# Attention scores of two heads at once, stacked at partitions 0 and 64, with a fourth bank for max scores

## The chip, the cores and the metric

The kernel runs on one core of one Trainium2 chip, in one launch. The metric is the device time in microseconds (us), taken as the median of several runs; lower is better.

## The reference

The input x is 8 batches of 512 tokens with 256 features. One transformer layer is computed in fp32: causal attention with 16 heads of size 16 beside a gated memory path, a layer norm, then a mixture of 8 experts (top 2 of 10, two of them null), and another layer norm. What the change touches is the attention alone:

```python
scores = jnp.einsum('bhtd,bhsd->bhts', q, k) * scale      # 8 batches, 16 heads, 512 x 512
scores = jnp.where(causal, -jnp.inf, scores)
attn = jax.nn.softmax(scores, axis=-1)
seq_out = jnp.einsum('bhts,bhsd->bhtd', attn, v)
```

## The kernel before

Three stages follow each other: an opening (weights, the first batch's projections, memory lines of all batches), eight attention batches, and a last stage with the experts.

**Stacks.** TensorE multiplies in a rounded type (fp32r). For fp32 accuracy each q and k is split in a high and a low part, and q·k is hi·hi + hi·lo + lo·hi. The parts are stacked along partitions: tile `Q` holds (hi, hi, lo) and tile `K` holds (hi, lo, hi), 3 x 16 = 48 rows of a head, zeros up to row 95 (`STACK = 96`), and in rows 96 and 97 `Q` has the row maxima (high and low part) and `K` has -1. One head is one matmul, with 96 rows (max scores) or 98 rows (exp scores, which subtract the maximum).

**Groups and units.** A batch is 4 groups of 4 heads; a group is 12 units (`unit_parts`, L285). Units 0 to 3 are one head with 512 key columns each, 4 to 7 one head with 384, 8 and 9 two heads with 256, 10 and 11 two heads with 128 (done as 256). Each unit is computed twice:

- `pe_max_scores` (L305) computes q·k with queries on partitions into one of three PSUM banks (`S_ps`, `u % 3`), and `dve_max` (L459) adds the mask and takes the row maximum. It may start unit u when unit u-3 has been read (`s_max`, L311). It runs 8 units (`LEAD`) plus one group ahead of the exp scores.
- The 16 columns of maxima of a group are turned by `pe_turn_max` (L354), split into high and low part by `dve_turned_max` (L483, tile `MT`), and written into rows 96 and 97 of `Q` by two DMAs (`sp_max_rows`, L640). The first exp unit of the group waits for them (`s_mrow`, L322).
- `pe_exp_scores` (L318) computes k·q into one of two banks (`ST_ps`, `u % 2`), and `act_exp` (L403) takes the exponential into `Pr`. It may start unit u when the exp of unit u-2 is done (L323). GpSimd masks the diagonal (`pool_mask`, L608), and `pe_values` (L331) multiplies with V for the group before, at units 0, 2, 4, 6. Its four heads go to four 32-column strips of the output and its operands are plain fp32.

**Beside it.** Each group carries two of the next batch's eight projection steps (`pe_project`, L360): six matmuls into bank `J_ps`, at units 4 and 10; `act_project` (L413) and `dve_project` (L473, at units 5 and 11) evacuate it. Steps 0 to 3 give q and k parts in the single tile `HL`, stored to DRAM (`sp_projected`, L620) and loaded back as stacks with six DMAs a group (`sp_stack`, L628); `act_project` writes `HL` only after the step before has been stored. Steps 4 to 7 give v and the memory value (`Vn`, `MV`). `act_out` (L424, unit 7), `pe_turn_out` (L343) and `dve_normalise` (L495), both at unit 10, finish the outputs of the group before. `act_split_x` and `dve_split_x` (L435, L508) split the next batch's x at unit 0 of group 0. From batch 2 to batch 6 VectorE also runs 36 scans of the memory path (`dve_scan`, L512), three in two groups of three (`SCAN_AT`, L548), at units 6, 8, 10 and then 0, 2, 4.

Every engine runs a list of its own in program order; they meet at semaphores alone. TensorE's order is `pe_batch` (L381): for each unit exp scores, max scores, values, project, turn max, turn out.

## Time and profile before

| | before |
|---|---|
| median of 3 runs | 833.69 us (831.81 to 835.61) |
| the profiled execution, device time | 833.96 us |
| its span, first to last instruction | 832.2 us |
| TensorE busy (modelled) | 745.5 us, 90% |
| VectorE busy | 592.8 us, 71% |
| ScalarE busy | 354.1 us, 43% |
| GpSimd busy | 443.3 us, 53% |
| mean granted TensorE clock | 0.936 of 2.4 GHz |
| opening / attention / last stage | 0 to 77.9 / 77.9 to 544.6 / 544.6 to 832.2 us |

The attention stage is counted from the first exponential of batch 0 to the end of the last exponential of batch 7. "Busy" of TensorE counts a matmul from its start to its modelled end; overlapping matmuls make it say little on pace, which is read from the distance between starts. PEld rows are weight loads. A row of the order of time gives start and length in us, then engine, line, operation, tiles, shape, and how many like instructions were merged (x2); in square brackets stands the engine's idle time before it and what ended that.

### The profile page before, as it was taken

Reading aid. Unit: us, or ns where it says so; the run is one execution under the profiler, and the core shown is the slowest. Engines: PE = TensorE matmul, PEld = TensorE weight load, DVE = VectorE, ACT = ScalarE, POOL = GpSimd, SP = SyncE. Lnnn points to the kernel's source line nnn. Section 1 sums busy time; section 2 is a strip of 40 time slices with the busy share of each in tenths; the row PEclk is TensorE's granted clock in tenths of the full one; section 3 lists DMA queues with packets and bytes.
Section 4 is the critical chain, followed back from the end, with each engine's and each line's share of the span. In section 5 each row is a group of like instructions: output and inputs, shape, how many; then the busy total and the mean of one; then the engine's idle time right before and its main releaser. Section 6 shows DMA issues by size and latency. Waiting matters only on the chain.

```text
span 832.2 us, 12627 instructions
## 1 busy us (share of the span) xinstructions
PE 745.5 (90%) x4116; PEld 519.1 (62%) x4116; DVE 592.8 (71%) x2089; ACT 354.1 (43%) x709; POOL 443.3 (53%) x350
## 2 busy tenths in 40 slices
PE   6994998998898999999889998878999999999995
PEld 3552665566465565565555664557788787887884
DVE  2344776778887888888788776635767777677685
ACT  2211555555454455555455465732242342332410
POOL 9200994995676666667475891524254153341510
PEclk9995999999998999999999996979999999999998
DMA  7899599574654655756564556030220302303000
GB/s 272 263 235 175 125 138 144 154 122 97 156 82 96 154 84 112 159 90 146 110 96 112 121 88 214 8 102 0 77 86 18 102 11 91 102 2 102 26 26 26
DMA packets 60421, 89.89 MB, mean 108 GB/s; under 512 B 8234, under 2 KB 37316, under 8 KB 60356
## 3 DMA queue, kind: packets, MB, share of 16 engines
q1 hardware_dynamic: 60356, 89.09, 47.5%
q8 instruction: 33, 0.54, 0.3%
q14 instruction: 32, 0.26, 0.1%
HBM read 54.72 MB, written 33.82 MB: 106 GB/s over the span
## 4 chain that ended last, share of the span: by engine, by line
PE 58%; DVE 18%; DMA 7%; POOL 6%; ACT 5%; issue 4%; SPq 2%; ACTq 0%; POOLq 0%; DVEq 0%
PE ps L1246 21%; PE ps L374 10%; PE ps L338 7%; PE ps L327 7%; PE ps L315 6%; DMA Q<-MT 5%; DVE ps L468 5%; DVE Ob L516 3%; PE ps L232 2%; PE ps L1212 2%; ACT X L1232 1%; DVE Z L1266 1%; ACT Pr L411 1%; PE ps L351 1%; DVE HL L477 1%
## 5 line engine op out<-in xcount | busy, mean ns | idle before, releaser
L468 DVE CUSTOM_DVE_ANT_0 ps<-ps,mask 128x256 f32<-128x256 f32 (+3 forms) x512 | 236.6, 509 | 29.4 <-PE ps L315 28.8
L411 ACT ACTIVATE Pr<-ps 128x512 f32<-128x512 f32 (+2 forms) x384 | 190.1, 527 | 112.3 <-PE ps L327 108.2
L327 PE MATMUL ps<-Q,K 98*128 98x256 f32 (+2 forms) x512 | 172.3, 379 | 27.2 <-DMA Q<-MT 20.0
L1246 PE MATMUL ps<-ew_hi,XT 128*128 128x512 f32 x512 | 181.4, 416 | 0.0
L315 PE MATMUL ps<-K,Q 96*128 96x256 f32 (+2 forms) x512 | 156.9, 352 | 23.2 <-DVE nmax L468 22.8
L1372 DVE SCALAR_TENSOR_TENSOR A<-ps,cw,A 128x256 f32<-128x256 f32 x256 | 123.6, 483 | 54.1 <-PE ps L1246 42.7
L327 PEld LDWEIGHTS ps<-Q,K 98*128 98x128 f32 x512 | 93.7, 196 | 102.0 <-ACT Pr L411 60.4
L612 POOL TENSOR_SCALAR_AFFINE_SELECT Pr<-Pr 128x512 f32<-128x512 f32 x128 | 88.6, 706 | 100.8 <-ACT Pr L411 98.4
L315 PEld LDWEIGHTS ps<-K,Q 96*128 96x128 f32 x512 | 101.6, 201 | 45.0 <-DVE nmax L468 28.6
L1246 PEld LDWEIGHTS ps<-ew_hi,XT 128*128 128x128 f32 x512 | 101.3, 198 | 21.8
L1246 PE MATMUL ps<-ew_rest,XT 128*128 128x512 f32 x256 | 104.8, 409 | 0.0
L338 PE MATMUL ps<-Pr,V 128*17 128x512 f32 (+3 forms) x1024 | 98.0, 458 | 1.7 <-POOL Pr L612 1.7
L1186 POOL TENSOR_TENSOR A<-A,X 128x512 f32<-128x512 f32 x16 | 20.6, 1287 | 94.8 <-ACT A L1238 94.8
L468 DVE DVE_READ_ACCUMULATOR2_ANT nmax<- 128x1 f32 x512 | 69.5, 136 | 0.0
L1246 PEld LDWEIGHTS ps<-ew_rest,XT 128*128 128x128 f32 x256 | 50.8, 198 | 9.4
L419 ACT ACTIVATE HL<-ps,qkb 128x512 fp32r<-128x512 f32 x32 | 22.0, 687 | 80.5 <-PE ps L374 55.8
L801 POOL TENSOR_TENSOR Ob<-Wm 128x511 f32<-128x511 f32 (+1 forms) x12 | 14.2, 1187 | 66.2 <-DMA Wm<-mem_scratch 66.0
L852 POOL TENSOR_TENSOR Ob<-Ob,Rl 128x1533 f32<-128x1533 f32 x12 | 34.8, 2903 | 27.4 <-DVE Ob L516 27.4
L374 PE MATMUL ps<-xhi,wqk 128*128 128x512 f32 x128 | 47.3, 454 | 1.8 <-DVE HL L477 1.5
L516 DVE TENSOR_TENSOR_SCAN Ob<-sc,Ob 128x512 f32<-128x512 f32 x36 | 45.7, 1269 | 0.0
L854 POOL TENSOR_TENSOR Wm<-Wm,Ob 128x1533 f32<-128x1533 f32 x12 | 43.3, 3609 | 0.9
L374 PE MATMUL ps<-wvc,xhi 128*128 128x512 f32 x128 | 42.8, 415 | 0.4 <-DVE bc L945 0.4
(187 smaller groups left out, 1115.8 us busy)
## 6 DMA issues: line engine op xcount, KB each, us to landing
qk_scratch<-HL SPq DMA_DIRECT2D x32, 512.0 KB, 3.2
Q<-qk_scratch SPq DMA_DIRECT2D x96, 128.0 KB, 4.3
K<-qk_scratch SPq DMA_DIRECT2D x96, 128.0 KB, 5.6
Pr<-xT SPq DMA_DIRECT2D x8, 512.0 KB, 6.0
xraw<-xT SPq DMA_DIRECT2D x8, 512.0 KB, 6.4
mem_scratch<-Rl SPq DMA_DIRECT2D x16, 256.0 KB, 6.6
mv_scratch<-MV SPq DMA_DIRECT2D x32, 128.0 KB, 1.7
Wm<-mem_scratch SPq DMA_DIRECT2D x16, 256.0 KB, 9.3
```

What stands on the lines that cost most here:

```text
L315: last = nc.tensor.matmul(o, Q[0:STACK, hh, P * i:P * i + P], K[0:STACK, hh, 0:n], start=True, stop=True)
L327: last = nc.tensor.matmul(o, K[0:STACK + 2, hh, P * kt:P * kt + P], Q[0:STACK + 2, hh, T - n:T], start=True, stop=True)
L338: last = nc.tensor.matmul(O_ps[32 * h:32 * h + VW, P * kt:T], V[:, kt, GROUP * g + h, :], probs(g % 2, kt, h, 1)[:, 0, :], start=(kt == 0) ...
L374: last = nc.tensor.matmul(J_ps[:], lhs, rhs, start=first, stop=(j < 4 and k == KT - 1 and a == 1))
L411: nc.scalar.activation(probs(g % 2, kt, heads[0], len(heads)), src, ACT.Exp, scale=SCALE).then_inc(s_exp, 1)
L468: last = nc.vector.tensor_tensor_reduce(out=scores, in0=scores, in1=mask[:, T - w:T], scale=1.0, scalar=NEG, op0=ALU.add, op1=ALU.max, acc ...
L516: nc.vector.tensor_tensor_scan(Ob[:, j % 3, :], col(SC_D).to_broadcast([P, T]), Ob[:, j % 3, :], 0.0, ALU.mult, ALU.add).then_inc(s_scan, 1)
L612: nc.gpsimd.affine_select(out=diagonal, in_=diagonal, compare_op=ALU.is_ge, fill=0.0, base=0, pattern=[[0, GROUP], [1, P]], channel_multip ...
L852: step(nc.gpsimd.tensor_tensor(Ob[:, :, 0:T - 1], Ob[:, :, 0:T - 1], Rl[:, i:i + 1, 1:T].to_broadcast([P, 3, T - 1]), ALU.mult))
L854: step(nc.gpsimd.tensor_tensor(Wm[:, lo:lo + 3, 0:T - 1], Wm[:, lo:lo + 3, 0:T - 1], Ob[:, :, 0:T - 1], ALU.add))
L1246: last = nc.tensor.matmul(o, lhs(c, k), rhs(d, k), start=first, stop=(k == KT - 1 and c == 1))
L1372: ins = nc.vector.scalar_tensor_tensor(acc, F_ps[v % 4][:, D * c:D * c + D], cw[:, par, i, e:e + 1], acc, ALU.mult, ALU.add)
```

## The change

- `STACK` becomes 48 and the zero rows go. `Q` and `K` hold two heads on top of each other: even heads at partitions 0 to 49, odd heads at partitions 64 to 113 (`HALF = 64`), each with its two rows of maxima at 48 and 49 of its half. The tiles have half as many columns. A new tile `later` is allocated ahead of them and not used in this stage.
- `pe_max_scores` and `pe_exp_scores` are called every second unit and issue two units u and u+1, one matmul from each half in turn, so that two neighbouring matmuls use different halves of the rows and different banks. Units 8 to 11 pair heads 0 and 2, 1 and 3.
- Max scores have four banks (0, 1, 7, 5). The turned output goes to the bank of `O_ps` and the turned maxima to that of `J_ps`; the waits follow the new owners: a project step waits for the copy of the turned maxima, the turned maxima for the end of the last project step, and the values of a group for the normalised output of the last.
- The exp scores of a pair wait until the exponentials of both units before it are done (`s_exp` of `UNITS * g + u`, where it was `u - 1`).
- Project steps are at units 0 and 8 (they were at 4 and 10), evacuated by ScalarE after units 1 and 9 and by VectorE at units 3 and 11. The turned output is at unit 8, ahead of the project step, and `dve_normalise` at unit 9; `dve_turned_max` is at unit 5.
- The split of x for batch b+2 is at the end of batch b (that of batch 1 ahead of batch 0).
- The DRAM layout of q and k has the parts inside the head. A projected tile is stored with two DMAs, high and low part apart. A group's stacks are loaded with eight DMAs (they were six), with the same bytes; its maxima with four (they were two).
- GpSimd's opening memsets cover 64 rows of `K` in place of 96 rows of `Q` and `K`.

```diff
-STACK = 96
+STACK = 48
+HALF = 64
-        S_ps, ST_ps = ps[0:2] + ps[7:8], ps[2:4]
-        O_ps, OT_ps, J_ps = ps[4:7]
-        M_ps = OT_ps
+        S_ps, ST_ps = [ps[0], ps[1], ps[7], ps[5]], ps[2:4]
+        O_ps, J_ps = ps[4], ps[6]
+        OT_ps, M_ps = O_ps, J_ps
...
+        def stacked(t, hh, n):
+
+            return t[HALF * (hh % 2):HALF * (hh % 2) + n, hh // 2, :]
...
         def pe_max_scores(pe, b, g, u):
...
             need(pe, s_max, PU, b, UNITS * g + u - 2)
-            for c, h in enumerate(heads):
-                hh = GROUP * g + h
-                o = S_ps[u % 3][:, c * 256:c * 256 + n]
-                last = nc.tensor.matmul(o, Q[0:STACK, hh, P * i:P * i + P], K[0:STACK, hh, 0:n], start=True, stop=True)
-            last.then_inc(s_s, 1)
+            for c in range(len(unit_parts(u)[1])):
+                for v in (u, u + 1):
+                    rank, heads = unit_parts(v)
+                    i, hh = QT - 1 - rank, GROUP * g + heads[c]
+                    n = max(P * (i + 1), 2 * P)
+                    ins = nc.tensor.matmul(S_ps[v % 4][:, c * 256:c * 256 + n], stacked(Q, hh, STACK)[:, P * i:P * i + P],
+                                           stacked(K, hh, STACK)[:, 0:n], start=True, stop=True)
+                    if c == len(heads) - 1:
+                        ins.then_inc(s_s, 1)
...
-            need(pe, s_exp, PU, b, UNITS * g + u - 1)
+            need(pe, s_exp, PU, b, UNITS * g + u)
...
-                for u in range(UNITS):
+                for u in range(0, UNITS, 2):
                     pe_exp_scores(pe, b, g, u)
                     on, ng, nu = ahead(g, u)
                     if not (last and on):
                         pe_max_scores(pe, b + on, ng, nu)
-                    if u in (0, 2, 4, 6) and not (first and g == 0):
+                    if u < 8 and not (first and g == 0):
                         pe_values(pe, pb, pg, u // 2)
-                    if u in (4, 10) and not last:
-                        pe_project(pe, b + 1, 2 * g + u // 10)
+                    if u == 8 and not (first and g == 0):
+                        pe_turn_out(pe, pb, pg)
+                    if u in (0, 8) and not last:
+                        pe_project(pe, b + 1, 2 * g + u // 8, NG * b + g + 1 + u // 8)
...
-                    if g == 0 and u == 0 and not last:
-                        act_split_x(act, b + 1)
-                    if u in (4, 10) and not last:
-                        act_project(act, b + 1, 2 * g + u // 10)
+                    if u in (1, 9) and not last:
+                        act_project(act, b + 1, 2 * g + u // 9)
+                    if (g, u) == (NG - 1, 10) and b < NB - 2:
+                        act_split_x(act, b + 2)
...
             for r in range(2):
-                sp.dma_start(Q[STACK + r:STACK + r + 1, GROUP * g:GROUP * g + GROUP, :].rearrange(
-                    "o h (i t) -> o (h i) t", i=QT).bitcast(F32), MT[:, g % 2, r, :].bitcast(F32)).then_inc(s_mrow[g], 16)
+                for a in range(2):
+                    row = HALF * a + STACK + r
+                    sp.dma_start(Q[row:row + 1, 2 * g:2 * g + 2, :].rearrange("o c (i t) -> o (c i) t", i=QT).bitcast(F32),
+                                 MT[2 * QT * a:2 * QT * a + 2 * QT, g % 2, r, :].bitcast(F32)).then_inc(s_mrow[g], 16)
```

## Rows read from the trace of the kernel before

**Rows 1.** Stretches (us, busy us by engine, clock, DMA share): batches 0, 1, 2 to 6, 7
```profile
core 0: us, PE busy (x) PEld busy (x) DVE busy (x) ACT busy (x) POOL busy (x), PEclk, DMA share, GB/s
77.93:133.80 55.87, 51.89 (x294) 35.06 (x293) 39.75 (x160) 30.10 (x61) 43.62 (x39) 0.92 0.78 134
133.80:191.02 57.22, 53.00 (x330) 33.90 (x328) 42.46 (x166) 30.64 (x62) 48.66 (x41) 0.97 0.69 130
191.02:489.42 298.40, 271.93 (x1642) 174.45 (x1640) 245.57 (x867) 154.21 (x310) 201.36 (x125) 0.95 0.57 115
489.42:544.57 55.15, 47.89 (x302) 27.49 (x304) 39.43 (x142) 35.99 (x72) 25.07 (x25) 0.85 0.41 105
```
**Rows 2.** Stretches: groups 0 and 2 of batch 6
```profile
430.34:447.65 17.31, 14.48 (x83) 9.04 (x81) 13.73 (x45) 9.40 (x18) 12.66 (x7) 0.90 0.45 86
...
463.48:476.44 12.96, 12.66 (x85) 8.37 (x83) 9.70 (x43) 6.96 (x16) 9.84 (x8) 1.00 0.63 114
```
**Rows 3.** TensorE's longest wait, attention stage: total us, times, longest us
```profile
PE ps L315 <- DVE nmax L468: 20.8, 36, 2.3
```
**Rows 4.** Order of time, batch 6 group 2: TensorE and ScalarE
```profile
463.55 1.05 PE L338 MATMUL ps<-Pr,V 128*17 128x512 f32 x8
...
464.53 0.19 PEld L327 LDWEIGHTS ps<-Q,K 98*128 98x128 f32 x1 [0.85 <-ACT Pr L411]
...
464.87 0.41 PE L315 MATMUL ps<-K,Q 96*128 96x256 f32 x2
...
465.06 1.08 ACT L411 ACTIVATE Pr<-ps 128x512 f32<-128x512 f32 x2 [0.99 <-PE ps L327]
...
465.11 0.40 PE L327 MATMUL ps<-Q,K 98*128 98x512 f32 x1
...
465.34 0.40 PE L315 MATMUL ps<-K,Q 96*128 96x256 f32 x2
...
465.67 0.13 PEld L338 LDWEIGHTS ps<-Pr,V 128*17 128x17 f32 x8
...
470.18 0.90 ACT L411 ACTIVATE Pr<-ps 128x384 f32<-128x384 f32 x2
...
471.07 0.19 PEld L327 LDWEIGHTS ps<-Q,K 98*128 98x128 f32 x1 [0.21 <-issue]
...
471.55 0.49 ACT L411 ACTIVATE Pr<-ps 128x384 f32<-128x384 f32 x1 [0.46 <-PE ps L327]
...
472.09 0.30 PEld L327 LDWEIGHTS ps<-Q,K 98*128 98x128 f32 x2 [0.19 <-ACT Pr L411]
...
474.98 0.48 PEld L351 LDWEIGHTS ps<-ident,Osb 128*128 128x128 f32 x4
...
475.43 0.30 PEld L327 LDWEIGHTS ps<-Q,K 98*128 98x128 f32 x2
```
**Rows 5.** Groups of instructions (busy us, mean ns, idle before), attention stage, ScalarE
```profile
L419 ACT ACTIVATE HL<-ps,qkb 128x512 fp32r<-128x512 f32 x28 | 19.2, 687 | 69.5 <-PE ps L374 53.0 <-DMA qk_scratch<-HL 16.5
L427 ACT ACTIVATE Osb<-ps 128x512 f32<-128x512 f32 x31 | 18.4, 592 | 0.0
...
L438 ACT ACTIVATE xhi<-xraw 128x1024 fp32r<-128x1024 f32 x7 | 7.3, 1049 | 0.0
```
**Rows 6.** Order of time, batch 6 group 0: the split of x on VectorE
```profile
433.47 2.63 DVE L510 TENSOR_TENSOR xlo<-xraw,xhi 128x1024 fp32r<-128x1024 f32 x1
...
437.03 0.47 PE L315 MATMUL ps<-K,Q 96*128 96x512 f32 x1 [2.30 <-DVE nmax L468]
```
**Rows 7.** TensorE's longest wait at the opening's end, 60 to 80 us
```profile
PE ps L327 <- DMA Q<-MT: 9.5, 1, 9.5
```
**Rows 8.** Order of time, batch 6 group 2: SyncE issues the maxima's DMAs
```profile
470.69 1.14 SPq L643 DMA_DIRECT2D Q<-MT  x2
```
**Rows 9.** The same DMAs in the whole attention stage: issue to landing
```profile
DMA to landing us min/median/max: 1.8/2.8/7.8
```

More of the change, by code:

```diff
@@ L217, in opening @@
                 project(j)
[L218 removed]
+                scores(*((0, 4), (4, 6), (6, 10), (10, 12))[j - 4])
             memory(16)
@@ L318, in pe_exp_scores @@
         def pe_exp_scores(pe, b, g, u):
-            kt, heads = unit_parts(u)
-            n = max(T - P * kt, 2 * P)
             if u == 0:
-                need(pe, s_mrow[g], 32, b, 32)
-            need(pe, s_exp, PU, b, UNITS * g + u - 1)
-            for c, h in enumerate(heads):
-                hh = GROUP * g + h
-                o = ST_ps[u % 2][:, c * 256:c * 256 + n]
-                last = nc.tensor.matmul(o, K[0:STACK + 2, hh, P * kt:P * kt + P], Q[0:STACK + 2, hh, T - n:T],
-                                        start=True, stop=True)
@@ L329, in pe_exp_scores @@
-            last.then_inc(s_st, 1)
+                need(pe, s_mrow[g], 64, b, 64)
+            need(pe, s_exp, PU, b, UNITS * g + u)
+            for c in range(len(unit_parts(u)[1])):
+                for v in (u, u + 1):
+                    kt, heads = unit_parts(v)
+                    hh = GROUP * g + heads[c]
+                    n = max(T - P * kt, 2 * P)
+                    ins = nc.tensor.matmul(ST_ps[v % 2][:, c * 256:c * 256 + n],
+                                           stacked(K, hh, STACK + 2)[:, P * kt:P * kt + P],
+                                           stacked(Q, hh, STACK + 2)[:, T - n:T], start=True, stop=True)
+                    if c == len(heads) - 1:
+                        ins.then_inc(s_st, 1)
@@ L364, in pe_project @@
             need(pe, s_lo, 8, b, j)
+            need(pe, s_mt, 2, turned, 0)
             first = True
@@ L730, in mem_rows @@
                         "(w h) t -> h w t", h=H)).then_inc(s_mw[c], 16)
-            opening(project, lambda i: sp_memory(sp, i), lambda: None, lambda u: None)
+            opening(project, lambda i: sp_memory(sp, i), lambda: None, lambda u0, u1: None)
             for i in range(6):
@@ L951, in project, with scores @@
                 dve_project(dve, 0, j)
-            def scores(u0):
+            def scores(u0, u1):
                 if u0 == 0:
-                    dve.wait_ge(s_cst, 2)
-                for u in range(u0, u0 + 3):
+                    dve.wait_ge(s_cst, 1)
+                for u in range(u0, u1):
                     dve_max(dve, 0, 0, u)
@@ L995, in fold @@
                 for k in range(KT):
-                    last = nc.tensor.matmul(OT_ps[:, 0:D], mb_bc[:, k, :], wst_ow[:, k, :],
+                    last = nc.tensor.matmul(S_ps[3][:, 0:D], mb_bc[:, k, :], wst_ow[:, k, :],
                                             start=(k == 0), stop=(k == KT - 1))
@@ L1011, in scores @@
                     pe.wait_ge(s_wr, 4)
-                for u in range(u0, u0 + 3):
+                for u in range(u0, u1, 2):
                     pe_max_scores(pe, 0, 0, u)
@@ L1018, in _ @@
             pe.wait_ge(s_p1g, 2)
-            pe_turn_max(pe, 0, 0)
-            for u in range(LEAD):
+            pe_turn_max(pe, 0, 0, 8)
+            for u in range(0, LEAD, 2):
                 pe_max_scores(pe, 0, 1, u)
```

112 lines of the change are left out of this document (58 added, 54 removed).

## The prediction

> **What bounds the kernel now.** I read the stretches first. The attention stage is 466.6 of the 832.2 us of span, and the change reaches little else. Its five middle batches take 298.40 us, 59.7 each; batches 0, 1 and 7 take 55.87, 57.22 and 55.15 [rows 1]. In a group that nothing disturbs TensorE is busy for 12.66 of 12.96 us and VectorE for 9.70, ScalarE for 6.96 [rows 2]. So a clean group is bound by TensorE's issue, and four of them would be 51.8 us. What is above that is stalls: 7.9 us in a middle batch, 5.4 in batch 1, 4.0 in batch 0, 3.3 in batch 7. Group 0 of batch 6, with 17.31 us, shows the kind [rows 2]. TensorE's largest wait there and in the stage as a whole is for VectorE's maxima to free a bank, 20.8 us in 36 waits [rows 3]. VectorE is busy for 245.57 of the 298.40 us of the middle batches, 49.1 us a batch, since the scans fall there [rows 1]: it is the second bound, close behind.
>
> Then I read one clean group in order of time for the pace of TensorE [rows 4]. Starts after a matmul of 512 columns are 0.23 us apart (465.11 to 465.34), two of 256 columns take 0.24 (464.87 to 465.11), 0.12 each. Where the array is empty the weight load shows: from the load at 464.53 to the next matmul at 464.87 is 0.34, so 0.11 of load and 0.23 of stream. The eight value matmuls, four heads in four column strips with plain fp32 operands, take 0.98 (463.55 to 464.53) and are in flight together: this is concurrency in the array, but of columns, not of rows. From the last score matmul (started at 465.34 + 0.12, 0.11 of stream) to the load for the values at 465.67 is 0.10, which I take as the drain when the use of the array changes.
>
> **What the change removes.** A group has 16 exp and 16 max matmuls: 4 of 512 columns, 4 of 384, 8 of 256 each. By the paces above, with 0.17 for 384 as the mean of its neighbours, that is 2 x (0.92 + 0.68 + 0.96) = 5.1 us. If two halves run at once it is 2.6. The trace of before has no row of two row halves. The nearest, the values, speak for full overlap; the other end is none. I take full overlap, of the weight loads too, and keep the other end for the range. The Trainium skill (TensorEngine Tiling (Array Packing), Tiling Modes) says that tiles of 64 rows load and multiply in parallel; by it the sum is the one I take.
>
> **What it adds: a lockstep.** Before, the exp scores of unit u waited for the exp of u-2, so TensorE filled one bank while ScalarE read the other. Now a pair waits for both exps of the pair before. Behind that wait stand max scores, values and project steps. So a group is six rounds, and each is the longer of two chains.
>
> ScalarE's chain: from the load to the start of the exp 0.53 (464.53 to 465.06), two exps of 512 in 1.08, and from the exp's end (471.55 + 0.49) to the next load at 472.09 another 0.05: 1.66 us. With 384 columns: 0.48 (471.07 to 471.55) + 0.90 + 0.05 = 1.43. Two of 256: exps of 512 and 384 are 0.60 and 0.49, so 0.38 each and 0.67 a pair is my estimate, 1.25 in all [rows 4].
>
> TensorE's chain rules where there is a project step. Round 0: load 0.11, one exp step 0.23, two max steps 0.24, drain 0.10, values 0.98, project 0.11 + 6 x 0.23 = 1.49, drain 0.10: 3.25. Rounds 2, 4, 6 have values and max scores in the shadow of ScalarE's 1.66, 1.43, 1.43. Round 8: the copy of the output on ScalarE 0.59 [rows 5], the turned output 0.45 (474.98 to 475.43) [rows 4], project 1.49, drain 0.10: 2.63. Round 10: 1.25. ScalarE's evacuation of a q or k step, 0.69 [rows 5], comes ahead of the exps in rounds 2 and 10 and outlasts the 0.53 by 0.16; that of v and memory values is half as wide and hides, but such a step has one more matmul, 0.12. Groups 0 and 1: 3.25 + 1.82 + 1.43 + 1.43 + 2.63 + 1.41 = 11.97. Groups 2 and 3: 3.37 + 1.66 + 1.43 + 1.43 + 2.75 + 1.25 = 11.89. The split on ScalarE, 1.05 [rows 5], now stands in round 10 of group 3, uncovered. A batch: 2 x 11.97 + 2 x 11.89 + 1.05 = 48.8 us where it was 51.8. So of 2.5 us of matmul time a group only 0.8 to 1.1 comes back; the rest is idle time in the lockstep.
>
> **The stalls.** (a) The split of x on VectorE, 2.63 us long, held up max scores, and TensorE lost 2.30 [rows 6], with the granted clock at 0.90 in that group (full is 2.4 GHz, the mean has stretches at 1.2) against 1.00 [rows 2]. It now comes ahead of a round of 3.25 us with two max pairs in store. I take 3.0 us a batch away, 2.0 in batch 0, where it moves into the wait of 9.5 us for the first maxima [rows 7]. If that cover is gone, it costs them again. (b) New: VectorE evacuates the project step of round 8 at unit 11, and TensorE wants the bank 1.7 us into the next group; `HL` must be stored before ScalarE writes it at unit 1, where it had until unit 4. Both are late when scans fall at units 6, 8, 10. (c) The maxima: four DMAs at 0.57 each in place of two (1.14 for two) [rows 8]. The turned maxima leave TensorE 3.25 + 1.82 + 1.3 = 6.4 us into a group; with 1.4 for VectorE the issues run from 7.8 to 10.1, and the last lands at 9.5 + 1.8 = 11.3 at best, at 12.3 with the median of 2.8 [rows 9], against a group of 12.0. (d) SP also issues eight stack loads for six, and two stores for one; only in group 1, where the stack waits for the last store, does that push the maxima. For (b) to (d) I take 1.3 us a batch. Below nothing they can't go; at worst they are the slower rival below. (e) The fourth bank and the earlier turned output can take from what is left of stalls; I put nothing for it.
>
> **The sum.** Middle batch: 48.8 + 7.9 - 3.0 + 1.3 = 55.0, five are 275. Batch 1: 48.8 + 5.4 - 3.0 + 1.3 = 52.5. Batch 0: 48.8 + 4.0 - 2.0 + 1.3 = 52.1. Batch 7 has no project steps, and its groups 1 and 2 stand behind other work; I take 51.4. Together 431, 35.6 less than 466.6. The opening ends on the DMA that brings the maxima [rows 7], which no TensorE saving moves; the split of storing `HL` may give 1 us. The last stage is the same. Against the profiled execution's 833.96 us (span 832.2, median 833.69): 797 us.
>
> **The rivals.**
> - *Half the gain.* Either the two weight loads of a pair go one after the other: 0.10 more for each pair of 384 or 256 columns and at each refill, some 0.65 a group where TensorE rules, 18 us, 815. Or VectorE sets the middle batches, since its 49.1 us a batch [rows 1] are not touched and it can't use all of its idle time: they stay at 59.7, 23 us more, 820. The Trainium skill speaks for the second (TensorEngine Tiling (Array Packing), Performance Considerations): tiling speeds up TensorE but not the evacuation of PSUM, which may become the bottleneck. For it: 82% busy already. Against: much of its idle time was behind project steps, ahead of which turned output and turned maxima now stand. 0.18.
> - *The change doesn't do what it says*: no overlap of row halves. Round 0 is 0.47 longer, round 8 0.41, rounds 2 and 4 some 0.25 each, 1.3 a group, 42 us; without new drains 7 us less: about 832. 0.08.
> - *Slower: the first exp of each group waits for the maxima's last DMA.* Place: the `s_mrow` wait. It decides from the point where that DMA lands more than 12.0 + 1.1 us into a group, 1.1 being the gain per group (36 us over 32). With landings of 4.2 us, between the median and the longest of 7.8 [rows 9], it lands at 13.7 in every group: 1.7 x 32 = 54 us, about 850. 0.12.
> - *Better*: the lockstep holds and the stalls nearly vanish, since turned maxima and output come earlier and a bank is added. Middle batches 51, the others 50: 405, 62 less, 771. 0.12.
>
> **How the numbers follow.** The forecast, 785 to 812, has 0.50. 0.5% is about what a measurement of this kernel can tell from no change, 4.2 us. Faster by more: 0.50 + 0.18 + 0.12 and a little of the no-overlap case, 0.81. Within: 0.05. Slower: 0.14. The range takes in better, half and no overlap: 770 to 834.
>
> **What would show it.** Right: neighbouring score matmuls of a pair start within some 10 ns; exp pairs wait for ScalarE about 0.3 to 0.6 us in rounds 2 to 6 and 10; a clean group of about 12.0 us; no 2.3 us wait behind the split of x. The serial rival shows starts in a pair 0.1 apart, no overlap 0.12 to 0.23. The slower one shows the wait for `Q<-MT` in most groups. The prediction is wrong if clean groups are well under 11.5 us (rounds overlap more than I hold) or if waits of VectorE or of the clock (granted under 0.9 over whole batches, since TensorE now idles in every round) grow beyond 8 us a batch.

## The result, and the profile after

| | before | after |
|---|---|---|
| median, runs one after the other on the same chip | 834.65 us (831.81 to 837.46, 4 runs) | 864.88 us (860.45 to 867.7, 4 runs) |
| ratio to before | 1 | 1.0365, 95% interval 1.031 to 1.0419 |
| span of the profiled execution | 832.2 us | 866.0 us |
| mean granted TensorE clock | 0.936 | 0.873 |
| opening, to the first exponential | 77.93 us | 87.04 us |
| attention stage | 466.6 us | 491.2 us |
| last stage | 287.6 us | 287.8 us |

The change made the kernel 3.65% slower, where I had forecast 797 us and a range that ended at 834. The loss has two places: 9.1 us in the opening and 24.6 in the attention stage. The last stage is the same. The medians and ratios below leave out those runs of a kernel that took over 1.5% longer than its fastest one.

The stretches of after, one line each for batches 0, 1, 2 to 6 and 7, then group 3 of batch 6 (nothing disturbs it) and group 1 of batch 6. The columns are those of [rows 1].

```profile
core 0: us, PE busy (x) PEld busy (x) DVE busy (x) ACT busy (x) POOL busy (x), PEclk, DMA share, GB/s
87.04:148.01 60.97, 48.08 (x296) 26.69 (x294) 39.10 (x160) 30.05 (x62) 44.70 (x39) 0.81 0.68 127
148.01:206.00 57.99, 47.62 (x332) 25.53 (x330) 42.44 (x169) 30.43 (x62) 49.20 (x41) 0.88 0.54 131
206.00:519.21 313.21, 251.17 (x1644) 135.57 (x1640) 245.06 (x865) 151.56 (x309) 198.40 (x125) 0.84 0.40 109
519.21:578.20 58.99, 43.12 (x301) 20.97 (x301) 40.55 (x139) 35.81 (x72) 25.75 (x25) 0.74 0.32 96
507.32:519.21 11.89, 10.69 (x87) 5.94 (x83) 9.28 (x42) 6.92 (x15) 11.74 (x5) 1.00 0.32 90
476.88:495.42 18.54, 13.77 (x85) 7.46 (x81) 13.20 (x45) 7.41 (x16) 8.26 (x6) 0.72 0.44 128
```

Against [rows 1] the middle batches went from 59.7 to 62.6 us each. Yet the clean group went from 12.96 [rows 2] to 11.89, what the round sums said (11.89; single rounds are off by up to 0.06 us, so the agreement to the hundredth is luck). So the gain of the pairs is there, and something outside the clean groups takes it back several times over. The granted clock is 1.00 in the clean group and 0.72 in group 1: a group with long waits also has stretches at 1.2 GHz, which [rows 2] already showed at 0.90.

The pairs themselves, in the clean group's order of time (start, length, engine, line; x2 are two neighbours merged; L343 exp scores, L328 max scores, L356 values, L388 the project step):

```profile
510.12 0.19 PEld L343 LDWEIGHTS ps<-Q,K 50*128 50x128 f32 x2 [0.26 <-issue]
510.13 0.51 PE L343 MATMUL ps<-Q,K 50*128 50x512 f32 x2
...
510.47 0.40 PE L328 MATMUL ps<-K,Q 48*128 48x256 f32 x4
...
510.66 1.09 ACT L426 ACTIVATE Pr<-ps 128x512 f32<-128x512 f32 x2
510.80 0.13 PEld L356 LDWEIGHTS ps<-Pr,V 128*17 128x17 f32 x8
```

Both weight loads of the pair together take the time of one (0.19, as one alone in [rows 4]), both matmuls begin with them, and the max scores follow 0.34 after the start of the pair. Two exp matmuls of 512 columns and four max matmuls of 256 are through in 0.67 us (510.13 to 510.80). The overlap of the row halves is complete.

What grew is in the waits. The longest of the kinds that concern the change, for the whole of after (engine and line that waited, for what: total us, times, longest us):

```profile
PE ps L343 <- ACT Pr L426: 65.7, 85, 4.2
ACT HL L434 <- DMA qk_scratch<-HL: 58.5, 13, 7.6
...
PE ps L343 <- DMA Q<-MT: 20.0, 7, 9.1
...
PEld ps L328 <- DVE nmax L487: 11.6, 11, 4.6
PE ps L388 <- DVE xlo L529: 10.1, 4, 4.3
```

And of before:

```profile
PEld ps L315 <- DVE nmax L468: 28.6, 52, 2.4
ACT HL L419 <- DMA qk_scratch<-HL: 24.7, 9, 3.8
...
PE ps L327 <- DMA Q<-MT: 20.0, 9, 9.5
PE ps L327 <- ACT Pr L411: 6.8, 20, 0.8
```

TensorE's wait for the exponentials has grown most, from 6.8 to 65.7 us. Most of it is the lockstep that the forecast counted on (with the store repaired, in *e1* below, it is still 47.1). ScalarE's wait for the store of `HL`, 24.7 us, has become 58.5. The matmuls' wait for the maxima's DMAs is the same 20.0, but that of the weight loads ahead of them (rows PEld) rose from 22.9 to 41.2. TensorE's loads wait 11.6 us for VectorE's maxima, which were 28.6. One new wait is for the low part of x, 10.1 us. The chain that ended last shows the store in its place; this is group 1 of batch 6 (start, length, what):

```profile
476.62 0.62 DVE HL L496
...
477.26 5.96 DMA qk_scratch<-HL
...
483.30 0.69 ACT HL L434
483.99 0.98 ACT Pr L426 x2
```

VectorE ends the low part of `HL` at 477.24. Its store, issued right then, lands after 5.96 us, and only then may ScalarE write `HL` for the next step. Behind ScalarE's write stand the exponentials, and in this version each pair of score matmuls waits for those. In before one store of 512 KB had a median of 3.2 us from issue to landing in this stage. Now there are two of 256 KB, and the second lands later than the one of double size did. Between 200 and 520 us the five longest pieces of the chain are all such landings, 4.27 to 6.11 us each.

### The profile page after: what moved, and what is told of

Read it like the earlier page. It is cut to its first block, busy times and chain, and to the rows that moved or that the text cites. A ratio compares the mean times of both kernels' runs of the same rounds, so it can differ in the third digit from the quotient of the medians.

```text
span 866.0 us, 12804 instructions
## 1 busy us (share of the span) xinstructions
PE 710.7 (82%) x4116; PEld 455.5 (53%) x4116; DVE 593.9 (69%) x2089; ACT 351.8 (41%) x709; POOL 428.9 (50%) x349
## 4 chain that ended last, share of the span: by engine, by line
PE 50%; DVE 18%; DMA 12%; ACT 9%; SPq 4%; issue 4%; POOL 3%; ACTq 0%; POOLq 0%; DVEq 0%
PE ps L1272 20%; PE ps L388 10%; DMA qk_scratch<-HL 7%; PE ps L343 6%; DVE ps L487 5%; ACT Pr L426 5%; PE ps L356 4%; DVE Ob L535 3%; PE ps L328 3%; DMA Q<-MT 2%; PE ps L1238 2%; PE ps L235 2%; SPq L660 2%; PE ps L364 2%; ACT X L1258 1%
## 5 line engine op out<-in xcount | busy, mean ns | idle before, releaser
L426 ACT ACTIVATE Pr<-ps 128x512 f32<-128x512 f32 (+2 forms) x384 | 182.9, 523 | 101.6 <-PE ps L343 96.9
L343 PE MATMUL ps<-Q,K 50*128 50x256 f32 (+2 forms) x512 | 103.3, 441 | 86.0 <-ACT Pr L426 65.7
L1398 DVE SCALAR_TENSOR_TENSOR A<-ps,cw,A 128x256 f32<-128x256 f32 x256 | 123.6, 483 | 54.1 <-PE ps L1272 42.7
L343 PEld LDWEIGHTS ps<-Q,K 50*128 50x128 f32 x512 | 48.7, 205 | 161.3 <-ACT Pr L426 78.1
L356 PE MATMUL ps<-Pr,V 128*17 128x512 f32 (+3 forms) x1024 | 108.1, 500 | 1.1 <-DVE On L522 1.1
L328 PE MATMUL ps<-K,Q 48*128 48x256 f32 (+2 forms) x512 | 82.1, 359 | 11.0 <-DVE nmax L487 8.5
L388 PE MATMUL ps<-xhi,wqk 128*128 128x512 f32 x128 | 57.7, 542 | 19.8 <-DVE xlo L529 10.1
L434 ACT ACTIVATE HL<-ps,qkb 128x512 fp32r<-128x512 f32 x32 | 22.0, 687 | 113.4 <-DMA qk_scratch<-HL 58.5
L328 PEld LDWEIGHTS ps<-K,Q 48*128 48x128 f32 x512 | 56.2, 213 | 17.8 <-DVE nmax L487 11.6
L388 PEld LDWEIGHTS ps<-xhi,wqk 128*128 128x128 f32 x128 | 30.1, 260 | 44.3 <-DVE HL L496 18.1
L388 PE MATMUL ps<-wvc,xhi 128*128 128x512 f32 x128 | 48.0, 459 | 3.3 <-DVE HL L496 1.5
L535 DVE TENSOR_TENSOR_SCAN Ob<-sc,Ob 128x512 f32<-128x512 f32 x36 | 45.6, 1267 | 0.0
```

Of the source, the lines that this page charges most:

```text
L328: ins = nc.tensor.matmul(S_ps[v % 4][:, c * 256:c * 256 + n], stacked(Q, hh, STACK)[:, P * i:P * i + P], stacked(K, hh, STACK)[:, 0:n], st ...
L343: ins = nc.tensor.matmul(ST_ps[v % 2][:, c * 256:c * 256 + n], stacked(K, hh, STACK + 2)[:, P * kt:P * kt + P], stacked(Q, hh, STACK + 2)[ ...
L356: last = nc.tensor.matmul(O_ps[32 * h:32 * h + VW, P * kt:T], V[:, kt, GROUP * g + h, :], probs(g % 2, kt, h, 1)[:, 0, :], start=(kt == 0) ...
L388: last = nc.tensor.matmul(J_ps[:], lhs, rhs, start=first, stop=(j < 4 and k == KT - 1 and a == 1))
L426: nc.scalar.activation(unit_probs(g % 2, kt, heads), src, ACT.Exp, scale=SCALE).then_inc(s_exp, 1)
L434: nc.scalar.activation(HL[:, 0, :], J_ps[:], ACT.Identity, bias=qkb[:, m:m + 1]).then_inc(s_hi, 1)
```

## The experiments

Four things are asked. Is it the form of the store? Do the row halves bring what the clean group says? What is the new order worth, step by step? And what holds the rest up? In each group the kernels ran beside before on the same chip, and a ratio stands against that. Where two kernels ran on different chips, their difference is taken from the ratios, times 833 us.

### The store of HL

*e1_one_store*: after, with the DRAM layout of before and one store, all else kept (the eight stack loads and the wait counts are fitted to the layout, and for k the high and the low part change places in `HL`).

```diff
-        qk_scratch = nc.dram_tensor("qk_scratch", [NB, 4, 8, 2, DH, T], F32, kind="Internal").ap()
+        qk_scratch = nc.dram_tensor("qk_scratch", [NB, 4, P, 2, T], F32, kind="Internal").ap()
-                for s, done in ((0, s_hi), (1, s_lo)):
-                    need(sp, done, 8, b, j + 1, apart=True)
-                    sp.dma_start(qk_scratch[b, j, :, s], HL[:, s].bitcast(F32)).then_inc(s_scr[j // 2], 16)
+                need(sp, s_lo, 8, b, j + 1, apart=True)
+                sp.dma_start(qk_scratch[b, j], HL[:].bitcast(F32)).then_inc(s_scr[j // 2], 16)
```

> The changed kernel with one part undone: q and k are stored in one DMA of 512 KB whose outermost dimension is the 128 partitions, as before the change, and the stacks are loaded from that layout (parts interleaved row by row, still eight loads of the same bytes). Theory 1, the stores are slow because their outermost dimension is 8: the store lands after about 2.7 us in place of 6, the opening is back at about 78 us (it was 87), ScalarE's wait for the store of HL falls from 58.5 us to about 10, and the time is 812 us (805 to 822). Rival, the lockstep of exp pairs with its idle time and lower clock is what costs: the kernel stays within 10 us of the changed one, 855 to 865.

Measured: 826.57 us (821.61 to 831.63, 7 runs) against 832.11 of before, ratio 0.9933 (0.989 to 0.9977). So 36 us of after hang on the store (1.0365 less 0.9933); one edit turns it from 3.65% slower to 0.7% faster. The time is still above the 805 to 822 that I had expected, so the store is not all that was wrong. The stack loads are no rival: their medians to landing are 2.7 to 3.1 us in after and 2.7 to 2.9 in e1. The first exponential is back at 77.05 us, and the wait falls to

```profile
ACT HL L434 <- DMA qk_scratch<-HL: 22.2, 9, 3.9
```

*e2_before_eight*: before, with the layout of after and its two stores, and nothing else of the change.

```diff
-                sp.dma_start(qk_scratch[b, j], HL[:].bitcast(F32)).then_inc(s_scr[j // 2], 16)
+                    sp.dma_start(qk_scratch[b, j, :, s], HL[:, s].bitcast(F32)).then_inc(s_scr[j // 2], 16)
```

> The kernel before with the changed kernel's DRAM layout and its two stores (high and low part apart, outermost dimension 8), nothing else. Theory 1: the stores land after 5 to 6 us, the opening is 7 to 9 us longer, and a few of the later steps wait: 850 us (843 to 858). Rival: the store is harmless by itself and hurts only in the changed order: 833 to 838.

*e3_before_two_stores*: before, with two stores too, but in its own layout, where the outermost dimension of each store has 128 entries and not 8. The edit reads the same, as `qk_scratch[b, j, :, s]` of `[NB, 4, P, 2, T]`.

> The kernel before with two stores of 256 KB (high and low part apart) into its own layout, 128 rows of 2 KB each. Theory 1, it is the outermost dimension of 8: no loss, 831 to 838 us, the low part lands after about 2.7 us or less. Rival, two DMAs with rows of 2 KB in place of one with 4 KB are what is slow: as the kernel with outermost dimension 8, some 850 us.

Measured: e2 866.32 us (864.51 to 872.11), ratio 1.0471 (1.0389 to 1.0554), more than either side had expected; e3 828.92 us (825.73 to 834.19), ratio 0.9963 (0.9928 to 0.9998). ScalarE's wait, first e2, then e3:

```profile
ACT HL L419 <- DMA qk_scratch<-HL: 60.0, 15, 5.9
```
```profile
ACT HL L419 <- DMA qk_scratch<-HL: 17.2, 7, 3.9
```

The cleanest comparison is in the opening, where the chain comes to the first landing by the same steps (`HL` by ScalarE, `HL` by VectorE, the store) in all four kernels. That landing, in before, e3, e2 and after:

```profile
15.89 2.62 DMA qk_scratch<-HL
```
```profile
16.46 2.15 DMA qk_scratch<-HL
```
```profile
16.11 5.04 DMA qk_scratch<-HL
```
```profile
16.93 5.13 DMA qk_scratch<-HL
```

Same bytes and same number of stores in e2 and e3: it is the layout with eight outermost entries that costs (5.04 against 2.15 us), alone 4.7% of the kernel before. Two stores cost nothing. In each pair the second store is issued about 0.8 us behind the first, so the 5 us are no price of 256 KB alone. The Trainium skill (DMA: Bandwidth & Descriptors, Why a DMA increments its semaphore by 16 and not by 1) says that the slowest dimension of each side is looked at, and that the largest number of engines up to 16 that divides both is taken: by that rule 8 in after and 16 in e3. These runs agree: the time is 2.3 times as long, and in the last microsecond before the landing the DMA engines are busy for a share of 0.46 in e2 (20 to 21 us) and 0.43 in after (21 to 22 us), where it is 0.91 during the landing in e3 (16.6 to 18.5 us). The two layouts also differ in how the rows lie beside each other in DRAM; no run holds that fixed. In e2 the stack loads read the other layout as well, and TensorE's wait for the maxima rose from 20.0 to 33.0 us. The loads land no later (medians of 4.3 and 5.5 us, in before 4.3 and 5.6); what part of e2's loss is still theirs, no run divides.

### The row halves

*e4_same_half*: e1, with the pairs formed of two heads of the same half (0 and 2, 1 and 3), one after the other. Banks, waits and order stay.

```diff
-            if u < 4:
-                return 0, [u]
+            if u < 8:
+                return u // 4, [(0, 2, 1, 3)[u % 4]]
...
-            for c in range(len(unit_parts(u)[1])):
-                for v in (u, u + 1):
+            for v in (u, u + 1):
+                for c in range(len(unit_parts(u)[1])):
```

> The first kernel of this set, but the two matmuls that follow each other come from the same half of the rows (heads 0 and 2, then 1 and 3), so that they can't run at once. Same instructions, same waits. Theory: matmuls of a pair start 0.12 to 0.23 us apart, a clean group goes from 11.9 to about 13.0 us, and the time is 25 to 45 us above the first kernel's. Rival, the lockstep hides it anyway: under 10 us above.

Measured: 860.58 us (856.87 to 865.53), ratio 1.035 (1.0281 to 1.0418); 34.0 us above e1, as expected (25 to 45). TensorE's rows in its clean group:

```profile
497.88 0.50 PE L341 MATMUL ps<-Q,K 50*128 50x512 f32 x1
497.88 0.50 PE L326 MATMUL ps<-K,Q 48*128 48x256 f32 x2
498.22 0.38 PE L341 MATMUL ps<-Q,K 50*128 50x512 f32 x1
498.44 0.39 PE L326 MATMUL ps<-K,Q 48*128 48x256 f32 x2
498.76 0.84 PE L354 MATMUL ps<-Pr,V 128*17 128x384 f32 x8
```

Here the same six matmuls need 0.88 us (497.88 to 498.76), not 0.67, and the second exp matmul comes 0.34 behind the first. By this trace matmuls of different halves pass each other even where the code did not pair them: the program has both exp matmuls (L341, one half) ahead of the max matmuls (L326, which begin with the other half in this round), yet the first of L326 starts at 497.88 together with the first of L341, and the second of L341 only at 498.22. The clean group is 12.62 against 11.84 us in e1:

```profile
494.89:507.51 12.62, 12.14 (x85) 7.24 (x84) 9.33 (x42) 6.92 (x15) 12.47 (x5) 1.00 0.27 85
```
```profile
463.66:475.50 11.84, 10.63 (x87) 5.95 (x83) 9.28 (x42) 6.92 (x15) 11.69 (x6) 1.00 0.31 91
```

0.78 us times 32 groups is 25 of the 34.0 us. The row halves do what they should.

### The lockstep and the places

*e6_unit_waits*: e1, in which exp score unit v waits only for the exp of v-2.

```diff
-            need(pe, s_exp, PU, b, UNITS * g + u)
             for c in range(len(unit_parts(u)[1])):
                 for v in (u, u + 1):
+                    if c == 0:
+                        need(pe, s_exp, PU, b, UNITS * g + v - 1)
```

> The version with one store, but each exp score unit waits only for the exp of two units before, as in the kernel before, instead of the pair waiting for both. It asks for the price of the lockstep. If the lockstep costs what the sum says (2.5 us of matmul time removed in a group, 0.8 to 1.1 of it come back), clean groups fall from 11.9 to 11.0 to 11.5 and the time to 805 to 820 us. Rival: the two matmuls of a pair no longer start together, so the overlap of the row halves is lost for the exp scores, clean groups stay at 11.9 or rise and the time is 828 to 845 us.

Measured: 825.73 us (820.72 to 830.79, 9 runs), ratio 0.992 (0.9892 to 0.9948). Beside e1's 0.9933 this is no difference that can be told, a result that neither expectation had. The clean groups of batch 6 take 11.53 and 11.73 us. Part of the reason is lost overlap: the exp pair at 463.08 takes 0.68 us from first start to last end, where a pair that starts together takes 0.50. The other part is what comes next in the chain of such a group. It is the path of the maxima: VectorE, four DMAs that SyncE issues one after the other (L670), and the landing of the last:

```profile
459.16 0.64 SPq L670
...
460.53 0.64 SPq L670
...
461.21 1.77 DMA Q<-MT
...
463.08 0.59 PE ps L344 x2
```

TensorE's wait for them is 31.6 us in 22 waits, in e1 25.9 in 11. So with the lockstep gone a clean group ends on the maxima, and fewer or earlier DMAs for them would be the next thing to try; no run here does.

*e5_unit_six*: e1, with the second project step of a group at unit 6 (ScalarE after unit 7, VectorE at unit 8).

```diff
-                    if u in (0, 8) and not last:
-                        pe_project(pe, b + 1, 2 * g + u // 8, NG * b + g + 1 + u // 8)
+                    if u in (0, 6) and not last:
+                        pe_project(pe, b + 1, 2 * g + u // 6, NG * b + g + 1 + u // 6)
```

> The version with one store, but the second project step of a group stands at unit 6 instead of unit 8, so that the two are six units apart in both directions and its HL has the time from unit 8 to unit 1 of the next group. Theory, that what is left above the forecast are the short couplings of step (b): ScalarE's waits for the store in the attention stage fall from 14.1 to under 4 us, TensorE's waits for the bank of the project steps go with them, the time is 812 to 820 us. Rival, that these waits only covered others (VectorE, the clock): the waits fall but the time stays at 825 to 832.

Measured: 865.66 us (864.97 to 871.02), ratio 1.0386 (1.0347 to 1.0425), 38 us above e1. Both my theory and its rival were wrong by far. ScalarE's wait for the store did fall (22.2 to 15.3 us), but a new one came up:

```profile
PE ps L388 <- DVE MT L511: 21.1, 27, 1.6
```

The turned maxima and the project steps share a bank in this change. At unit 6 the project step stands behind VectorE's copy of the turned maxima, and that behind all maxima of the group; the chain of its clean group shows it:

```profile
518.10 0.14 DVE MT L509
...
518.27 0.29 DVE MT L511
...
518.70 1.63 PE ps L388 x6
```

So TensorE is tied to VectorE's newest result once a group. That it then lacks the lead for the scans would explain why 38 us are lost where these waits sum to 21.1; it is not shown.

*e9_own_bank* and *e10_own_bank_six*: e1 and e5, each with three banks for max scores, and the turned maxima in the bank that comes free.

```diff
-        OT_ps, M_ps = O_ps, J_ps
+        OT_ps, M_ps = O_ps, ps[5]
...
-            need(pe, s_max, PU, b, UNITS * g + u - 2)
+            need(pe, s_max, PU, b, UNITS * g + u - 1)
...
-            pe.wait_ge(s_lo, projected)
```

> The version with one store, but with three banks for max scores, and the turned maxima in a bank of their own instead of that of the project steps, so that neither waits for the other. It weighs the fourth bank against the shared one. Theory, that the sharing costs little while the second project step stands at unit 8, three units behind the turned maxima: TensorE waits more for VectorE's maxima (9.4 us before) and the time is 829 to 836 us. Rival, that the fourth bank is worth nothing and the sharing costs: 820 to 826.

> The version with the second project step at unit 6, again with three banks for max scores and the turned maxima in a bank of their own. At unit 6 that step waited for VectorE to copy the turned maxima out of the shared bank (18.70 in the chain of group 3 of batch 6), and with it all of TensorE stood behind VectorE. If this is what made unit 6 cost 37 us more than unit 8, the own bank gives most of it back: 825 to 840 us. Rival, that it is the place itself (project and evacuation in the chain between the exps of units 6 and 8, behind the copy of the output): 855 to 870 as before.

Measured (medians; the four kernels make a table):

| | second project step at unit 8 | at unit 6 |
|---|---|---|
| four banks for maxima, turned maxima share | e1 826.57 (ratio 0.9933) | e5 865.66 (ratio 1.0386) |
| three banks, turned maxima have their own | e9 848.66 (ratio 1.0156, 1.0097 to 1.0215) | e10 859.47 (ratio 1.0275, 1.0205 to 1.0346) |

At unit 8 three banks with the own one are 19 us slower, more than either side had expected. So the fourth bank is worth about 19 us there, or more if the own bank helps. TensorE's wait for VectorE's maxima shows it, e1 first, then e9:

```profile
PE ps L328 <- DVE nmax L487: 9.4, 12, 4.0
```
```profile
PE ps L328 <- DVE nmax L485: 24.1, 23, 2.3
```

At unit 6 the own bank brings 9 us on balance; if the fourth bank is worth 19 there too, the sharing costs about 28. With the own bank unit 6 is still 11 us worse than unit 8 (859.47 against 848.66). So of the 38 us some 28 would be the shared bank and 10 the place itself. That division rests on the fourth bank being worth the same in both places, which no run shows. The time itself fell in the range of e10's rival (855 to 870), because the bank that was given up hid what the own bank gave.

*e7_six_split_early* and *e8_all*: e5 with the split of x moved up from units 10 and 11 to 8 and 9, and that with the waits of e6.

```diff
-                    if (g, u) == (NG - 1, 11) and b < NB - 2:
+                    if (g, u) == (NG - 1, 9) and b < NB - 2:
                         dve_split_x(dve, b + 2)
```

> As the version with the second project step at unit 6, and the split of x moved up with it: ScalarE's part from unit 10 to unit 8 and VectorE's from unit 11 to unit 9 of group 3, ahead of the scan at unit 10. If TensorE's waits for the low part of x (10.9 us, four of them, up to 4.5) come from the scans ahead of the split, they fall under 4 us and the time is 5 to 7 us below that version's. Rival: VectorE sets the pace of these groups, the 2.6 us of the split hold up the maxima instead, and the time is the same within 2 us.

> All three edits at once: one store, the second project step at unit 6, the early split of x, and waits by unit. If the three costs are separate, the gains add: 795 to 808 us. If VectorE sets the middle batches (49.1 us a batch of its own work, with idle time that it can't use), they stay at 56 us or more and the time at 815 or more.

Measured: e7 857.62 us (ratio 1.0311, 1.0259 to 1.0363), e8 842.24 (1.0113, 1.0054 to 1.0171). The early split brings 8 us where 5 to 7 were expected, and the wait for the low part of x is gone from e7's list, though the intervals of e5 and e7 touch. The waits by unit bring 15 on this base, where on e1 they brought about 1: the price of the lockstep hangs on what else holds the groups up. e8 is far from its forecast of 795 to 808 and in the range of its rival (815 or more).

*e11_old_order*: e1's pairs and store with the order and banks of before (project steps at 4 and 10, split of x at unit 0, three banks, turned maxima and output in one bank).

```diff
+                    if u in (4, 10) and not last:
+                        pe_project(pe, b + 1, 2 * g + u // 10)
...
+                    if g == 0 and u == 0 and not last:
+                        act_split_x(act, b + 1)
```

> The pairs alone: one store, two heads at once on the two halves of the rows, but the order and the banks of the kernel before (project steps at units 4 and 10, turned maxima and turned output in one bank, three banks for max scores, x split at the first unit of a batch). If the new order brought what the sum says (3 us a batch from the split of x), this version is slower than the one with one store: 840 to 855 us. Rival, that the pairs give the gain and the new order only costs: 805 to 825.

Measured: 877.33 us (873.49 to 882.24), ratio 1.0526 (1.046 to 1.0591). That is worse than either side had expected. The pairs in the old order are 43 us slower than before itself, and 49 slower than in the new order. TensorE waits for VectorE's maxima for

```profile
PE ps L328 <- DVE nmax L491: 50.7, 55, 5.4
```

where before had 22.8 in all. A pair takes two banks at once, so three banks hold one pair and a half. Of the 49 us the third bank alone is some 19 (e9 against e1); the rest is order, places and the other bank sharing together. The lockstep stayed in e11, so what the pairs do in the old order without it is open.

### VectorE

*e13_short_scans* and *e14_before_short_scans*: e1 and before, with the scans of the memory part cut to 8 of 512 columns. The rest of the scan, and with it the memory part of the output, is left out.

```diff
-            nc.vector.tensor_tensor_scan(Ob[:, j % 3, :], col(SC_D).to_broadcast([P, T]), Ob[:, j % 3, :], 0.0,
+            nc.vector.tensor_tensor_scan(Ob[:, j % 3, 0:8], col(SC_D).to_broadcast([P, 8]), Ob[:, j % 3, 0:8], 0.0,
```

> The version with one store, with the 36 scans on VectorE cut to 8 columns (most of the scan is left out, so the memory part of the output is not computed). It takes 45.8 us of work off VectorE in the five middle batches and leaves all else. If VectorE's work sets these batches (244.6 of 286.2 us busy), they fall from 57.2 to 50 to 52 us a batch and the time to 795 to 805 us. Rival, that couplings and DMAs set them: they stay at 55 or more and the time at 818 or more.

> The kernel before, with the scans cut to 8 columns in the same way. It tells how much of the gain of the pairs the scans take. If the scans hold up both kernels alike, this one falls by as much as the version with one store does, to about 803 to 810 us, and the pairs bring 0.5 to 1% again. If the kernel before is held by TensorE's issue and the version with one store by VectorE, this one falls by only 10 to 15 us, to 818 to 823, and the pairs then bring 2 to 3%.

Measured: e13 799.52 us (795.68 to 802.54), ratio 0.9628 (0.958 to 0.9676); e14 814.99 us (812.63 to 815.51), ratio 0.9794 (0.9749 to 0.984). The first is as expected, the second lies between its two expectations. The scans cost e1 25 us and before 17. The middle batches, first e1 and then with short scans:

```profile
189.33:475.50 286.17, 231.53 (x1644) 125.23 (x1640) 244.57 (x865) 151.29 (x309) 202.75 (x126) 0.92 0.38 119
```
```profile
188.19:447.86 259.67, 222.04 (x1644) 120.30 (x1640) 203.90 (x865) 151.09 (x310) 196.51 (x127) 0.95 0.43 131
```

A batch falls from 57.2 to 51.9 us, with 8.1 us less work on VectorE in it. Without scans the pairs bring 15 us (814.99 to 799.52), with scans 5.5. So the scans on VectorE take most of what the pairs give. VectorE is not full (85% in e1); its work comes in lumps (three scans of 1.27 us each, and a split of 1.2 to 3.4 us), and TensorE's lead doesn't reach over them. That it is the lumps and their order is borne out by e12 below, which does the same work as e6 in another order and is 16 us faster. The clean sum was 48.8, so some 3 us a batch are left for other causes.

*e12_early_split*: e6, with VectorE's part of the second project step at unit 10 instead of 11, and the split of x ahead of the scan at unit 10.

```diff
-                    if (g, u) == (NG - 1, 10) and b < NB - 2:
+                    if (g, u) == (NG - 1, 9) and b < NB - 2:
                         act_split_x(act, b + 2)
...
-                    if u in (3, 11) and not last:
-                        dve_project(dve, b + 1, 2 * g + u // 11)
+                    if u in (3, 10) and not last:
+                        dve_project(dve, b + 1, 2 * g + u // 10)
...
-                    if (g, u) == (NG - 1, 11) and b < NB - 2:
+                    if (g, u) == (NG - 1, 10) and b < NB - 2:
                         dve_split_x(dve, b + 2)
```

> The version with one store and waits by unit, with VectorE's part of the second project step at unit 10 instead of 11 and the split of x at ScalarE's unit 9 and VectorE's unit 10 of group 3, both ahead of the scan at unit 10. In the version with one store TensorE waits 10.9 us for the low part of x, in four waits of up to 4.5 us, where three scans of 1.27 us stand ahead of the split. If the waits come from that place, most of them go: 817 to 822 us, 1.3 to 2% under the kernel before. Rival, VectorE has no room for it anywhere, and the split holds up the maxima for the same time: 825 to 828.

*e15_evac_ten*: e1 with the second of these edits alone; and e12 once more beside it.

> The version with one store, with one edit: VectorE's part of the second project step stands at unit 10 instead of 11. It divides the gain of the version with the early split (808.7, against 826.1 for waits by unit alone) between the earlier store of HL and the earlier split of x. If the bank of the project step and the store set the later groups, this alone brings 8 to 12 us: 816 to 821. Rival, the split of x has nearly all of it: 825 to 829.

> The version with the early split again, on this chip, to stand beside the one that moves VectorE's part alone: 806 to 811, as it was (808.7).

Measured: e12 808.7 us (805.84 to 810.99, 6 runs), ratio 0.9727 (0.9689 to 0.9766), and again 807.24 us (805.2 to 808.44), ratio 0.9704 (0.9672 to 0.9737); e15 819.11 us (817.38 to 829.02), ratio 0.9884 (0.9808 to 0.996). This is the fastest version that computes everything, 2.7 to 3.0% under before and 53 to 55 us under after; it beat its forecast of 817 to 822. e15 fell in the range of its theory, but its interval overlaps e1's (0.989 to 0.9977), so the earlier evacuation alone is not shown to bring anything; it is 12 us behind e12 on the same chip. Those 12 us belong to the split and the waits by unit together. The wait for the low part of x, e1 first:

```profile
PE ps L388 <- DVE xlo L529: 10.9, 4, 4.5
```
```profile
PE ps L389 <- DVE xlo L530: 3.7, 4, 1.4
```

Nearly all of e1's wait is two waits of 4.5 us, at the ends of batches 2 and 5, the only ones with scans at units 6, 8 and 10 of group 3. There the split itself takes 3.36 us; the median of all six is 1.91. In e1 the order on VectorE at such a place was (L535 the last of three scans, L529 the split, L388 the project step that needs it):

```profile
246.94 1.22 DVE L535 TENSOR_TENSOR_SCAN Ob<-sc,Ob 128x512 f32<-128x512 f32 x1
...
248.87 3.36 DVE L529 TENSOR_TENSOR xlo<-xraw,xhi 128x1024 fp32r<-128x1024 f32 x1
...
252.29 1.22 PE L388 MATMUL ps<-xhi,wqk 128*128 128x512 f32 x2 [4.53 <-DVE xlo L529]
```

## Why the prediction was wrong, step by step

- *The overlap and the clean group: right.* The loads lie together, the pair starts together, the drain is about as read. The forecast for groups 2 and 3 was 11.89; after has 11.90 and 11.89. e4 puts the price of losing the overlap at 34.0 us, where the rival of no overlap had 42 less 7.
- *The store of `HL`, steps (b) and "the split of storing HL may give 1 us": wrong, and this is the cause of the wrong sign.* The prediction took two stores of 256 KB as no slower than one of 512 KB, took 1 us off the opening for them, and put 1.3 us a batch for (b) to (d) together, without a row for the landing of a store. It knew the new layout, but not what its outermost dimension of 8 would cost. In the chains one landing takes 4.27 to 6.11 us in after; in the opening it takes 5.13, in before 2.62. It cost 36 us of the 68 between 797 and 864.88, by the ratios. Of the profiled executions, whose spans differ by 43.8 us, 10.0 us lie in the opening (87.04 against 77.05 in e1) and 34.0 in the attention stage (491.2 against 457.2). In the attention stage it came just where (b) had put the danger, on ScalarE's write of `HL` at unit 1: that wait rose from 16.5 to 42.8 us there. The other coupling of (b), TensorE's wait for the bank of the project steps, came too, with 11.1 us (L388 for `HL`). Of what is left with one store, e1's profile against the sum has 11 us in the middle batches, 12 in batches 0 and 7, and 3 in batch 1.
- *The stalls, step (a): wrong in place.* I let the split of x vanish behind a round of 3.25 us. But VectorE reaches it behind three scans at the ends of batches 2 and 5, and there TensorE waits 4.5 us for the low part (in e1; 4.3 in after). I named the condition ("if that cover is gone, it costs them again") and did not look at which scans stand in group 3. In e12, where the split goes ahead of the scan, the middle batches are 54.1 us:

```profile
188.22:458.84 270.62, 241.16 (x1644) 130.79 (x1641) 241.61 (x866) 150.62 (x309) 204.09 (x128) 0.94 0.41 126
```

  against 55.0 forecast and 57.2 in e1. That this comes near the sum is in part luck, since e12 has no lockstep and the sum has one.
- *Steps (c) and (d), the maxima's four DMAs: about right in after.* TensorE's matmuls waited 20.0 us for them, as before; in e1, where the store no longer covers it, 25.9. One term was too small: the four issues take 2.7 us (2.71 at 472.39 us), not 4 x 0.57. The slower rival (about 850 us) is nearest to the measured time, but by luck: its sign, the wait in most groups, did not come (7 waits of the matmuls, 20 of the loads), and e1 shows another cause.
- *Step (e), the fourth bank: mis-sized.* I put nothing for it; e9 says about 19 us. Without it the version with one store is slower than before (1.0156). That is what its loss costs in the new order; what it would add to before, no run shows.
- *The rival that VectorE sets the middle batches* (820 us) is the one whose mechanism showed, once the store is repaired: e1 has 826.57, and its middle batches take 57.2 us, between the 55.0 of the forecast and the 59.7 of the rival. (The 832 of the no-overlap rival is as near, but e4 rules that cause out.) e13 bears it out, and e12 adds that the order of VectorE's lumps decides, not its sum. The sentence of the Trainium skill (TensorEngine Tiling (Array Packing), Performance Considerations) that the prediction had set beside it, that PSUM's evacuation may become the bottleneck, fits e9, where TensorE waits 24.1 us for the maxima instead of 9.4; what e13 took away were scans, which evacuate nothing.
- *Batches 0 and 7*: in e1 they take 57.1 and 58.75 us, where I had 52.1 and 51.4. Together they miss 12 us. In both the granted clock is low (0.86 and 0.71 in e1, 0.92 and 0.85 in [rows 1]). Batch 7's line in e1:

```profile
475.50:534.25 58.75, 44.11 (x301) 21.73 (x301) 40.27 (x139) 35.92 (x72) 23.72 (x25) 0.71 0.31 96
```

  Whether the clock fell since the pairs leave TensorE more idle, or what else delays batch 7, no run here settles; it stays open.
- *The clock*: the prediction had named a granted clock under 0.9 over whole batches as a sign of being wrong, and the middle batches of after have 0.84. With the same matmuls it is 0.92 in e1 and 0.95 with short scans, so it followed the waits in these runs. What part of the 36 us of the store is the lower clock and what part is waiting, no run divides.

## What to carry to other kernels

When a change touches a DRAM layout, write down for each DMA the outermost dimension on both sides, not only bytes and rows: with 8 instead of 128 entries the same two stores took 5.04 us to land instead of 2.15. A gain in matmul time is only as large as the lead that TensorE has over the next engine's longest lump; before costing a step at nothing behind another engine, list what stands ahead of it in that engine's own order, in every batch that differs. And banks are worth their count in pairs once work is issued in pairs.

## What was new on the hardware

Two fp32 score matmuls on the two halves of the rows, 50 and 48 rows deep, run fully side by side, weight loads included (a pair of 512 columns and four of 256 in 0.67 us, where pairs from one half take 0.88). In the trace of e4 a matmul of the other half also starts ahead of one that the program put before it (L326 at 497.88, the second L341 at 498.22). Two stores of 256 KB with eight outermost entries landed 5.04 us after the second was issued, with 128 entries 2.15 us, and two of the latter cost the kernel nothing against one of 512 KB (ratio 0.9963).
